# A mixture-of-experts stage: weight requests tied to the splits instead of to the result stores

## The reference

```
x = x + tanh(g_xattn) * mlstm(layernorm(x), ctx, ctx, ...)      # 8 x 512 tokens, 1024 wide
x = x + tanh(g_ffn)   * ffn(layernorm(x), ...)
ffn: probs = softmax(flat @ router_w.T); the 2 best of 16 experts per token
     shared = (silu(flat @ sg) * (flat @ su)) @ sd              # 1024 wide inside
     routed = sum over the token's 2 experts of weight * (silu(x @ gate[e]) * (x @ up[e])) @ down[e]
     return shared + routed                                     # experts: 1024 -> 512 -> 1024
```

## Time and profile before

| what | before |
|---|---|
| median of 3 runs | 2996.3 us (2995.6 to 2996.47) |
| the profiled execution | 2988.89 us |
| its span, first to last instruction | 2987.3 us |
| TensorE busy, matmuls | 2781.5 us, 93% of the span |
| VectorE, ScalarE, GpSimd busy | 64%, 34%, 33% |
| mean granted TensorE clock | 0.973 |
| chain that ended last: PE, DMA, DVE, ACT | 40%, 10%, 5%, 4% |

### The profile page before, as it was taken

One profiled execution on the slowest core, in us unless ns is written; L12 is line 12 of the kernel. 1 busy time (PEld: TensorE's weight loads), 2 busy tenths in 40 slices (PEclk: granted clock), 3 DMA queues, 4 the chain that ended last, 5 costly groups with the idle time before them and its releaser, 6 DMA issues.

```text
span 2987.3 us, 49030 instructions
## 1 busy us (share of the span) xinstructions
PE 2781.5 (93%) x17030; PEld 2266.5 (76%) x17031; DVE 1916.6 (64%) x2873; ACT 1022.1 (34%) x1948; POOL 983.1 (33%) x1148
## 2 busy tenths in 40 slices
PE   3799999999999986999999999999999999999999
PEld 3677777787777765877777777777778778888887
DVE  3787878888887745555455545545555647666676
ACT  4444444444445412333233323323333321111111
POOL 1344433444444424433333343333333311111111
PEclk7799999999999988999999999999999999999999
DMA  6555455454454443453454454454454336666665
GB/s 200 143 171 162 149 166 161 157 178 150 156 171 158 136 153 134 138 179 127 171 173 169 171 178 172 169 176 170 172 179 174 112 141 189 201 191 191 199 181 182
DMA packets 292526, 496.52 MB, mean 166 GB/s; under 512 B 102032, under 2 KB 171536, under 8 KB 289680
## 3 DMA queue, kind: packets, MB, share of 16 engines
q1 hardware_dynamic: 116976, 333.62, 33.0%
q10 hardware_dynamic: 140544, 88.10, 10.7%
q0 software_dynamic: 34880, 73.10, 7.9%
HBM read 378.10 MB, written 134.45 MB: 172 GB/s over the span
## 4 chain that ended last, share of the span: by engine, by line
PE 40%; DMA 10%; DVE 5%; ACT 4%; issue 2%; ACTq 1%; POOL 0%; SPq 0%; DVEq 0%; POOLq 0%
PE p_y_b L1592 14%; PE p_g_b L1606 13%; PE p_up_b L1606 13%; DMA mid_h<-h_b 6%; DMA h_b<-mid_h 3%; ACT w_hi L1363 3%; DVE w_lo L1441 2%; DVE h_t_b L1458 1%; DVE ht_lo_b L1463 1%; DVE th_b L1486 1%; ACT ht_hi_b L1387 1%; DVE h_b L1490 1%; ACT th_b L1425 1%; DMA xn<-mid_xn,idx_q 1%; DVE x_t_b L1474 0%
## 5 line engine op out<-in xcount | busy, mean ns | idle before, releaser
L1307 POOL DMA_INDIRECT xn<-mid_xn,idx_q x284 | 295.7, 1041 | 564.5 <-DVE x_t_b L1474 471.7
L1592 PE MATMUL p_y_b<-w_hi,ht_hi_b 128*128 128x512 f32 x840 | 341.3, 406 | 62.8 <-DVE ht_lo_b L1463 62.8
L1606 PE MATMUL p_g_b<-w_hi,xt_hi_b 128*128 128x512 f32 x840 | 329.6, 392 | 22.1 <-DVE xt_lo_b L1480 16.9
L1458 DVE STREAM_TRANSPOSE h_t_b<-h_b 128x512 f32<-128x512 f32 x104 | 115.5, 1110 | 360.0 <-DMA h_b<-mid_h 359.1
L1592 PE MATMUL p_y_b<-w_hi,ht_lo_b 128*128 128x512 f32 x840 | 336.2, 400 | 0.0
L1592 PE MATMUL p_y_b<-w_lo,ht_hi_b 128*128 128x512 f32 x840 | 335.5, 399 | 0.0
L1606 PE MATMUL p_g_b<-w_lo,xt_hi_b 128*128 128x512 f32 x840 | 329.0, 392 | 1.0
L1606 PE MATMUL p_up_b<-w_hi,xt_hi_b 128*128 128x512 f32 x840 | 327.4, 390 | 0.0
L1606 PE MATMUL p_up_b<-w_hi,xt_lo_b 128*128 128x512 f32 x840 | 327.4, 390 | 0.0
L1606 PE MATMUL p_g_b<-w_hi,xt_lo_b 128*128 128x512 f32 x840 | 327.4, 390 | 0.0
L1606 PE MATMUL p_up_b<-w_lo,xt_hi_b 128*128 128x512 f32 x840 | 327.2, 390 | 0.0
(11 more groups left out here) (223 smaller groups left out, 5593.2 us busy)
## 6 DMA issues: line engine op xcount, KB each, us to landing
mid_y<-y_b SPq DMA_DIRECT2D x73, 512.0 KB, 3.3
stage<-mid_g_row SPq DMA_DIRECT2D x64, 512.0 KB, 5.4
stage<-in_eg SPq DMA_DIRECT2D x16, 2048.0 KB, 8.5
stage<-in_eu SPq DMA_DIRECT2D x16, 2048.0 KB, 15.2
stage<-in_ed SPq DMA_DIRECT2D x16, 2048.0 KB, 9.9
mid_h<-h_b ACTq DMA_DIRECT2D x104, 256.0 KB, 2.5
h_b<-mid_h ACTq DMA_DIRECT2D x104, 256.0 KB, 2.7
mid_y<-in_x SPq DMA_DIRECT2D x34, 512.0 KB
```

Of the source, the lines that this page charges most:

```text
L1307: nc.gpsimd.indirect_dma_start(out=xg_parts[:, n, :], out_offset=None, in_=xn_flat, in_offset=bass.IndirectOffsetOnAxis(ap=idx_q[:, n:n + ...
L1458: nc.vector.transpose(h_t[:, :, :].rearrange("p k (j t) -> p t k j", t=4), h[:, :].rearrange("p (t i k) -> p t k i", t=4, k=FE // P)).then ...
L1592: last = nc.tensor.matmul(p_y[n][:, :], a[:, k, :], b[:, GUP + k, w], start=(k == 0 and m == 0), stop=(k == FE // P - 1 and m == 2))
L1606: mm = nc.tensor.matmul(out[:, :], a[:, k, :], w[:, k, o:o + FE], start=(k == 0 and m == 0), stop=(k == KD - 1 and m == 2))
```

## The change

In SP's list of an expert the loads no longer stand behind stores of results. The gate and up weights of the next expert are the first item: they wait only for the splits of the present ones. Then comes the store of the old expert's last tile, then the down weights, which wait for the present down splits, then the stores of all other tiles but the last, the first tile's among them. At the very beginning the down weights of expert 1 go ahead of the store of tile 0. `start` loses an argument that served the store of the first tile alone.

```
-            return eng.value_load(starts_i[0:1, less, bass.ds(e, 1)], min_val=MIN_TILES - less,
-                                  max_val=MAX_TILES - left - less)
+            return eng.value_load(starts_i[0:1, less, bass.ds(e, 1)], min_val=MIN_TILES - less, max_val=MAX_TILES - less)
...
             def store_expert(e, after):
 
+                load_gate_up(after)
                 store_routed(start(sp, e, 1))
-                load_gate_up(after)
-                store_routed(start(sp, e, 0, MIN_TILES))
                 load_down(after)
-                with sp.Fori(start(sp, e) + 2, start(sp, e + 1)) as i:
+                with sp.Fori(start(sp, e) + 1, start(sp, e + 1)) as i:
                     store_routed(i - 1)
 
             load_gate_up(1)
+            load_down(1)
             store_routed(0)
-            load_down(1)
```

More of the change, by code:

```diff
@@ L1190, in tiles, with start @@
             finish(n + NCH, n + (NCH - 1), NE, NCH)
-        def start(eng, e, less=0, left=0):
-            return eng.value_load(starts_i[0:1, less, bass.ds(e, 1)], min_val=MIN_TILES - less,
-                                  max_val=MAX_TILES - left - less)
+        def start(eng, e, less=0):
+            return eng.value_load(starts_i[0:1, less, bass.ds(e, 1)], min_val=MIN_TILES - less, max_val=MAX_TILES - less)
         xn_quarters = t["xn"].rearrange("(c j t) (a d) -> c a j t d", t=4, j=32, a=4)
```

## The result

The changed kernel is slower: 3048.6 us median (3041.8 to 3049.8, 4 runs) against 2996.0 (2990.3 to 2996.5, 4 runs), a ratio of 1.0175 with a 95% interval of 1.0156 to 1.0195. That is +53 us, where +36 was forecast. The profiled execution took 3041.8 us (before 2988.9), its span is 3040.2.

A forecast was written before the change was run, and what follows sets the result against it. TensorE's wait for h through DRAM before the down projection was taken to bound. 1.9 us more idle plus 0.5 us slow matmuls, 15 times, gave +36 us: 3032 us (3025 on the profile's scale), full range 2982 to 3056.

The forecast's parts named there:

- What bounds, what moves, what is queued where: TensorE's wait for h before the down projection bounds; gate and up requests move 13.4 us earlier; queued result store costs nothing.
- h's company: Weight transfers beside h's store and load in DRAM: 9.6 us of their 14.92 us in the kernel before.
- when the load lands: First tile's h load lands at 1339.6, about level with the down weights; TensorE then idles 5.35 us, against 3.45.
- the sign to look for: In the profile after, TensorE's wait of p_y on ht_lo rises from 60.9 to about 90 us.
- The upper bound: Down weights land at most 22.4 us after the gate request, the time from request to landing in the kernel before.
- the nearest row: First tile's h store under gate and up weights takes 8.46 us, as the second tile's did; bounds 2.5 and 10.1.
- the first rival: First tile's h load slips in ahead of the down weights: faster, 2974 us, down to 2960; chance 0.18.
- The slow matmuls: The 24 down-projection matmuls after TensorE's stop run partly at 1.2 GHz: +0.5 us per request, bounds 0 and 1.1.
- usual: 5.73 us for 24 down-projection matmuls, against 7.07 after the stop in the kernel before.
- The second: TensorE's stall moves by one tile and keeps its length: 2996 us, within 6 us; chance 0.12.
- the third: SP reaches the weight request late, held by a result store; chance small, counted within that of no change.
- The first request: Expert 1's down weights ahead of store 0 move away from an x gather: 0 to 5 us gain, taken as nothing.

## Why the prediction was right, and where it was off

The forecast named the sign, the mechanism and the place. By its own steps, its times shifted by the expert's 2.84 us:

| step | forecast us | measured us |
|---|---|---|
| gate weights requested | 1320.74 | 1320.75 |
| h stored | 1326.51 | 1326.51 |
| down weights requested | 1334.94 | 1334.77 |
| store landed, load issued | 1334.99 | 1336.32 |
| down weights landed | 1341.8 to 1343.1 | 1344.6 |
| load landed | 1342.4 | 1344.86 |
| TensorE goes on | 1345.1 | 1347.59 |
| idle | 5.35 | 7.78 |

*What bounds, what moves, what is queued where*: right. The request is 0.17 us behind the eighth split (1313.69 + 6.89 = 1320.58). The second tile's stall is gone, the weights' earlier arrival bought nothing, the result store cost nothing. That the loss is due to h's company, and to nothing else in the change, is shown by the run with the down weights behind h: 2937 us.

*The term that was mis-sized is when the load lands*. The forecast let it land 21.7 us after the gate request (1317.9 to 1339.6). Measured, the down weights land 23.2 us after that request by the median of the 15 (before 22.4), and the load 0.3 us behind them (0.1 to 0.4), which is the forecast's own figure for a load that stands behind. That is 1.8 us more, and so is the idle: 7.17 us on average over the 15 stops against 5.35. (The expert shown is at the long end, 7.78.) As the 15 stops of before are 3.81 us on average and not the 3.45 of the one expert, the net is (111.1 - 60.9) / 15 = +3.35 us where +1.9 was forecast; the sign to look for was a wait of about 90 us, and it is 111.1.

The upper bound, 22.4 us, supposed that the weights pass with full engines, as before. Traffic from the gate request to the landing of the load, 22.71 us before and 24.11 now:

```profile
DMA packets 3506, 8.39 MB, mean 370 GB/s; under 512 B 306, under 2 KB 818, under 8 KB 3378
...
DMA packets 3377, 7.87 MB, mean 326 GB/s; under 512 B 304, under 2 KB 816, under 8 KB 3249
```

Fewer bytes pass, as forecast, but at a lower rate, so the engines were not full throughout. A likely cause stood in the forecast's own times and was not counted: the down weights are asked for 14.2 us behind gate (1317.9, 1332.1; measured 14.0) instead of 12.47 (1331.29, 1343.76). Whether that is all of it, no run separates. The store, put at 8.46 us by "the nearest row", took 9.42 by the median; as the load lands right behind the weights, that moved the margin of the first rival more than the sum.

*The slow matmuls* were put at +0.5 us per expert, 7.5 in all. Measured is +1.6 for the whole kernel: the 24 matmuls behind the stop take 7.4 us by the median, before 7.3. (The forecast's "usual" 5.73 us is an expert's first tile; most groups take 5.44, which the sum does not use.) In the expert shown the granted clock did stay low, at 0.50 where it was 0.68 in the earlier trace rows (last columns: granted clock, DMA share, GB/s):

```profile
1343.41:1346.82 3.41, 0.00 (x0) 0.00 (x0) 1.18 (x2) 0.71 (x2) 0.00 (x0) 0.50 0.05 21
1346.82:1350.23 3.41, 2.64 (x6) 2.15 (x7) 3.38 (x4) 1.10 (x3) 0.00 (x0) 0.50 0.00 0
```

but the first of these two stretches at 0.50, which is 1.2 GHz, fell into the idle time and cost nothing. The two errors partly cancelled, +36 against +53.

*The first rival* (the load slips in ahead) was not what happened, yet its condition was drawn rightly: it is decided by a few tenths. With the load 0.2 us ahead, the changed kernel is 1.3% faster than before, not 1.75% slower (the rival had put it at 0.7%). The forecast got its side of this edge from the store's duration, with a margin of 0.05 us (1332.1 against 1332.15), and the true one lay further on that side. That much of the sign was luck. *The second* (no change) needed a shorter trip and got a longer one; *the third* did not occur.

*The first request* (down weights of expert 1 ahead of store 0) was taken as nothing and was not run alone. The wait of 5.2 us for x rows is not in the list after.

The Trainium skill's rule ("DMA: Bandwidth & Descriptors", "Queues, rings and completion order"), that an engine takes turns between queues packet by packet, does not give the changed kernel its time: the load landed behind the weights. It agrees in kind with the run of 2 KB packets, where the load waits less long. What turn-taking does not tell is what weighs most here, who came first: 0.2 us ahead or 1.55 behind made 2.6 or 8.5 us.

## What to carry to other kernels

A bulk load that nobody waits for can still set the time, by what it does to a small transfer that somebody does wait for. Place bulk requests by when the engines carry nothing urgent, not by when their buffer comes free: here a wait on the small transfer in front of 2 MB took 82 us off a kernel in which those 2 MB were never late. And when two halves of a change touch one shared resource, run them apart: here one gave 58 us, the other cost 13 alone and 110 on top of the first.

## What the runs showed of the hardware that was not expected

- A 256 KB load issued on ScalarE's queue 0.20 to 0.24 us ahead of a 2 MB load on SP's takes 2.6 to 3.7 us; issued 0.11 to 1.93 us behind it, 7.6 to 10.1 us, landing 0.1 to 0.4 us after it. Here different queues did not shield a small transfer from a large one that was asked for first.
- A 256 KB store (512-byte packets) asked for 6.2 us behind 2 MB of down weights, themselves queued behind gate and up, took 13.18 us and landed with them. Where only gate and up, in 2 KB packets, were ahead of it, it took 9.57 (gate and up early alone), and 2.5 by the stage's median. Whether the bytes ahead of it or their packets of 16 KB made the difference is not shown.
- In the run with down weights early alone, SP's issue of the down weights directly behind gate and up took 3.32 us instead of 0.36 (1.28 to 4.70 us over the 15 requests):

```profile
1338.48 3.32 SPq L1120 DMA_DIRECT2D stage<-in_ed  x1
```
